# An RWKV block and an FP4 feed-forward on one Trainium2 core: chunks of 256 instead of 512 tokens

## The chip, the cores and the metric

The kernel runs on one core of a Trainium2 chip. The metric is the device time of one launch in microseconds (us). Several executions are timed and their median is given; one further execution is recorded by the hardware profiler.

## The reference

4,096 tokens (16 sequences of 256) go through three layers, all in fp32. `x` holds token numbers below 31,999; the lookup `w0[inputs]` is clipped to the 8,000 rows.

```python
# embedding
emb = einsum('blk,kh->blh', w0[inputs], w1) * (inputs != 0) * 256**0.5      # w0 8000x512, w1 512x256
# attention-like layer (D = 256, FF = 1024), after an extra layer norm of its input
h = layer_norm(x); hx = token_shift(h)
k, v, r = (h*mix + hx*(1-mix)) @ wk, wv, wr ; r = sigmoid(r)
wkv = scan over the 256 tokens of a sequence, two numerators and a running maximum
x = x + (r * wkv) @ wo
h = layer_norm(x); hx = token_shift(h)
kk = square(relu(mixed_k @ cwk)); rr = sigmoid(mixed_r @ cwr)
x = x + rr * (kk @ cwv)
# feed-forward with blockwise FP4 rounding of activations and weights, I = 704
xn = layer_norm(x)
x = x + fp4(silu(fp4(xn) @ fp4(w_gate).T) * (fp4(xn) @ fp4(w_up).T)) @ fp4(w_down).T
```

Every block of 16 values is scaled by its largest value and rounded to the 8 magnitudes of FP4.

## The kernel before

The tokens are cut into 8 chunks of 512 (two sequences, 4 tiles of 128 rows). A chunk passes three stages. Stage **a** gathers rows by indirect DMA (POOL, L429), transposes them (L497), multiplies by `w1` (L509), normalises (statistics on VectorE L949/L952, coefficients on POOL L434 to L458, application on ScalarE), transposes again (L519), forms the shifted mixes (ScalarE L744, then VectorE L963), projects to k, v, r (L537) and runs the recurrence: VectorE's scans and products (`wkv_a`, L970 to L1074, steps `a_wkv1` to `a_wkv4`) between ScalarE's relu, exp and ln (`exponentials`, L770). Stage **b** multiplies by `wo` (L557), adds (L1082), normalises, mixes, splits the key input into a high and a low fp32r part (L813, L1097), does the key matmul in three fp32r passes of 512 columns (L573), relu and square (L825, L828), gate (L835) and value (L588, run by L546). Stage **c** normalises, rounds to FP4 (`quantise`, L337: seven VectorE passes, of which the fifth, L362, waits for a square that ScalarE makes after the fourth, L358), transposes (L601), does gate and up in fp32r (L615), Silu and product (L859, L1145), rounds again, transposes (L629) and multiplies by the down weights (L642, the last 64 of 704 rows as a block of its own).

Each engine executes its own queue in order, and semaphores tie the queues together. The order of each queue is written by hand as a table `ORDER` (L67): a list of (step, lag). `walk` (L121) goes through the table once per chunk and calls each step for chunk t minus its lag; a stage-c step of chunk i thus stands beside stage-a steps of chunk i+2 or i+3. PSUM banks are handed out in a fixed cycle of jobs (`Jobs`, L131), two banks for each stage. Most tiles exist once; `h1` and the row numbers exist twice. At the start the weights of gate, up and down are themselves rounded to FP4 on VectorE (`quant_w`, L1165, three steps), transposed and split, among the first chunks' steps.

ScalarE has one table of functions at a time. Sigmoid, Silu, Exp and Ln each come with ACT_TABLE_LOAD instructions in the profile (53 in the chunks).

Of the kernel before, what the change touches and what calls it, by code (L numbers as in the profile page):

```python
# [26 lines left out]
F32 = mybir.dt.float32  # L27
F32R = mybir.dt.float32r
# [6 lines left out]
P = 128  # L35
# [8 lines left out]
GP = 88  # L44
GJ = INTER // GP
KI = 6
TAIL = INTER - (KI - 1) * P
BLOCK = 16
TOKENS = SEQS * T
CHUNK = 512  # L50
CHUNKS = TOKENS // CHUNK
NT = TOKENS // P
TILES = CHUNK // P
CS = CHUNK // T
# [5 lines left out]
AHEAD = 2  # L60
# [32 lines left out]
class Chunk:  # L93
# [15 lines left out]
class Signal:  # L109
# [6 lines left out]
    def count(self, ch, n):  # L116

        return ch.times(self.per, AHEAD * self.per + n)


def walk(name, steps):  # L121

    lags = [lag for order in ORDER.values() for _, lag in order]
    for t in range(min(lags), CHUNKS + max(lags)):
        for step, lag in ORDER[name]:
            ch = Chunk(t - lag)
            if ch.exists() and not (step[0] == "w" and ch.base > 0):
                steps[step](ch)


class Jobs:  # L131


    def __init__(self, jobs, full, emptied):
        self.names, self.who = [n for n, _ in jobs], [w for _, w in jobs]
        self.full, self.emptied = full, emptied

    def slot(self, name):
        return self.names.index(name) % 2

    def emptied_by(self, k):

        return self.emptied[self.who[k]], sum(w == self.who[k] for w in self.who[:k + 1])

    def wait_free(self, pe, ch, name):

        k = self.names.index(name) - 2
        signal, n = self.emptied_by(k % len(self.names))
        pe.wait_ge(signal.sem, signal.count(ch if k >= 0 else ch.back(1), n))

    def wait_full(self, engine, ch, name):

# [1076 lines left out]
```

## Time and profile before

| | |
|---|---|
| time of 3 runs, median (lowest to highest) | 788.66 us (787.74 to 792.24) |
| profiled execution: time, span in the trace | 790.58 us, 788.8 us |
| mean granted TensorE clock | 0.952 of full speed |
| busy: TensorE, its weight loads, VectorE, ScalarE, POOL | 89%, 72%, 76%, 65%, 19% |
| DMA moved | 19.34 MB, 25 GB/s mean |
| chain that ended last | TensorE 69%, VectorE 15%, ScalarE 7%, issue 6%, DMA 2% |

Busy time is time in which an engine has an instruction in execution. Matmuls overlap, so the distance between their starts, not their duration, is what a matmul costs. On VectorE and ScalarE two instructions that don't depend on each other overlap by some tens of nanoseconds, while one that needs the result of the one before starts after its end. The chain lists, in order of time, the pieces of work that each released the next.

### The profile page before, as it was taken

To read this page: it belongs to the slowest core of one execution; us is meant where nothing else is said; L and a number is where in the kernel's file an instruction comes from. 1 tells how busy PE (TensorE), PEld (TensorE's weight loads), DVE (VectorE), ACT (ScalarE), POOL (GpSimd) and SP (SyncE) were. 2 spreads that over 40 slices of the span, in tenths; PEclk is the share of its full clock that TensorE was granted. 3 is DMA by queue.
4 is the path that set the end of the run, shared out by engine and by line. 5 is a ranking of instruction groups with operands and counts; after the bars stand their busy time and mean duration, and the time that the engine had idled before them with its cause. 6 is when DMAs were issued, how large, how long until landed. Compare 5 with 4: busy or idle time off the path is not lost.

```text
span 788.8 us, 9882 instructions
## 1 busy us (share of the span) xinstructions
PE 698.7 (89%) x3311; PEld 566.1 (72%) x3311; DVE 600.1 (76%) x1023; ACT 511.7 (65%) x889; POOL 147.8 (19%) x220
## 2 busy tenths in 40 slices
PE   3353699699999999999999999999999999799686
PEld 2231576589688977888688958897789778688574
DVE  0797835987788888788788778888878888863763
ACT  1267488668874887389757886588748974761221
POOL 2042230433023300421022302330131003100000
PEclk9677799899999999999999999999999999899988
DMA  5800000000010000100010001000100000000000
GB/s 133 230 27 25 3 27 0 28 1 27 1 41 14 26 3 14 41 1 27 14 34 8 28 14 27 15 28 0 35 20 1 1 14 15 1 0 14 15 0 27
DMA packets 11956, 19.34 MB, mean 25 GB/s; under 512 B 972, under 2 KB 9346, under 8 KB 11906
## 3 DMA queue, kind: packets, MB, share of 16 engines
q1 hardware_dynamic: 9302, 10.31, 4.5%
q0 software_dynamic: 2560, 8.39, 3.7%
q8 instruction: 27, 0.44, 0.2%
q14 instruction: 23, 0.19, 0.1%
q10 hardware_dynamic: 44, 0.01, 0.0%
HBM read 14.51 MB, written 4.19 MB: 24 GB/s over the span
## 4 chain that ended last, share of the span: by engine, by line
PE 69%; DVE 15%; ACT 7%; issue 6%; DMA 2%; POOL 0%; SPq 0%; DVEq 0%; ACTq 0%; POOLq 0%
PE psB L546 17%; PE psB L573 11%; PE psC L642 11%; PE psC L615 11%; PE psA L537 9%; PE psA L509 3%; PE psC L629 3%; ACT mix L796 2%; DMA kkT<-L_ffn_w_gate 2%; DVE top L352 1%; DVE mix L1082 1%; PE psB L519 1%; PE psA L519 1%; DVE top L949 1%; ACT take L790 1%
## 5 line engine op out<-in xcount | busy, mean ns | idle before, releaser
L546 PE MATMUL psB<-cwv_s,kkT 128*128 128x256 f32 x512 | 113.2, 379 | 0.0
L546 PEld LDWEIGHTS psB<-cwv_s,kkT 128*128 128x128 f32 x512 | 96.6, 190 | 16.0 <-issue 3.7
L642 PE MATMUL psC<-downT,hqT 128*128 128x256 f32 (+1 forms) x384 | 97.0, 398 | 0.0
L429 POOL DMA_INDIRECT rows<-L_tok_w,ids_now x32 | 45.7, 1427 | 266.7 <-PE psA L497 255.1
L615 PE MATMUL psC<-up_hi,xq_hi 128*128 128x352 f32 x256 | 88.3, 345 | 7.4 <-DVE xq_lo L1194 6.8
L642 PEld LDWEIGHTS psC<-downT,hqT 128*128 128x128 f32 (+1 forms) x384 | 70.2, 193 | 26.7 <-issue 19.0
L537 PE MATMUL psA<-mix,kvr_s 128*128 128x512 f32 x192 | 86.8, 596 | 1.5 <-DVE mix L963 1.3
L615 PE MATMUL psC<-up_hi,xq_lo 128*128 128x352 f32 x256 | 84.0, 328 | 0.0
L615 PE MATMUL psC<-up_lo,xq_hi 128*128 128x352 f32 x256 | 83.9, 328 | 0.0
L537 PEld LDWEIGHTS psA<-mix,kvr_s 128*128 128x128 f32 x192 | 35.8, 190 | 41.1 <-issue 38.4
L963 DVE SCALAR_TENSOR_TENSOR mix<-hT,rest,mix 128x512 f32<-128x512 f32 x80 | 54.3, 747 | 10.3 <-ACT mix L744 10.3
L509 PE MATMUL psA<-w_s,rowsT 128*128 128x256 f32 x256 | 61.2, 395 | 0.0
L615 PEld LDWEIGHTS psC<-up_hi,xq_hi 128*128 128x128 f32 x256 | 49.3, 193 | 10.1 <-DVE xq_lo L1194 8.0
L573 PE MATMUL psB<-key_hi,cwk_hi 128*128 128x512 f32 x128 | 54.3, 424 | 1.9 <-ACT rr L835 1.9
L509 PEld LDWEIGHTS psA<-w_s,rowsT 128*128 128x128 f32 x256 | 50.6, 201 | 7.1
L362 DVE SCALAR_TENSOR_TENSOR hq<-square,hq 128x704 f32<-128x704 f32 x32 | 28.6, 893 | 35.1 <-ACT square L873 35.1
L744 ACT ACTIVATE mix<-hT,par 128x512 f32<-128x512 f32 x80 | 51.1, 734 | 0.2
L573 PE MATMUL psB<-key_lo,cwk_hi 128*128 128x512 f32 x128 | 50.7, 396 | 0.0
L573 PE MATMUL psB<-key_hi,cwk_lo 128*128 128x512 f32 x128 | 50.6, 395 | 0.0
L615 PEld LDWEIGHTS psC<-up_hi,xq_lo 128*128 128x128 f32 x256 | 49.3, 192 | 0.8
L546 PE MATMUL psB<-wo_s,rT 128*128 128x256 f32 x128 | 34.1, 415 | 17.1 <-DVE rT L985 17.1
L615 PEld LDWEIGHTS psC<-up_lo,xq_hi 128*128 128x128 f32 x256 | 49.2, 192 | 0.0
(163 smaller groups left out, 1435.6 us busy)
## 6 DMA issues: line engine op xcount, KB each, us to landing
out<-h SPq DMA_DIRECT2D x16, 256.0 KB, 2.1
mix<-L_attn_cwk SPq DMA_DIRECT2D x1, 1024.0 KB, 15.7
cwv_s<-L_attn_cwv SPq DMA_DIRECT2D x1, 1024.0 KB, 16.0
kkT<-L_ffn_w_gate SPq DMA_DIRECT2D x1, 704.0 KB
kkT<-L_ffn_w_up SPq DMA_DIRECT2D x1, 704.0 KB
hqT<-L_ffn_w_down SPq DMA_DIRECT2D x1, 704.0 KB, 17.9
w_s<-L_tok_w SPq DMA_DIRECT2D x1, 512.0 KB, 4.0
rows<-L_tok_w,ids_now POOLq DMA_INDIRECT x32, 4.1
```

Of the source, the lines that this page charges most:

```text
L362: op = nc.vector.scalar_tensor_tensor(out=data, in0=w.bitcast(F32), scalar=MAGIC, in1=data, op0=ALU.add, op1=ALU.add)
L429: pool.indirect_dma_start(rows[:, q, :], None, tok_w0, bass.IndirectOffsetOnAxis(ap=ids_now[:, s, t:t + 1], axis=0)).then_inc(rows_in[q], 16)
L509: mm = nc.tensor.matmul(psA[:, A.slot(f"e{j}"), q * D:(q + 1) * D], rowsT[:, q, k, :], w1_s[:, k, :], start=(k == 0), stop=(k == KE - 1))
L519: mm = nc.tensor.transpose(ps(jobs.slot(name))[:, t * P:(t + 1) * P], src[:, t, d * P:(d + 1) * P], ident[:])
L537: mm = nc.tensor.matmul(psA[:, A.slot(f"{name}{d}")], kvr_s[:, w, k, d * P:(d + 1) * P], mix[:, w, k].rearrange("p c t -> p (c t)"), start ...
L546: mm = nc.tensor.matmul(psB[:, B.slot(name), q * D:(q + 1) * D], lhsT[:, k, (2 * j + q) * P:(2 * j + q + 1) * P], weight[:, k, :], start=( ...
L573: mm = nc.tensor.matmul(psB[:, B.slot(f"kk{m}")], a[:, k, m * P:(m + 1) * P], b[:, k], start=(k == 0 and p == 0), stop=(k == H - 1 and p = ...
L615: mm = nc.tensor.matmul(psC[:, C.slot(name), f, 0:INTER // 2], a[:, k, t * P:(t + 1) * P], b[:, w, k, f * (INTER // 2):(f + 1) * (INTER // ...
L629: mm = nc.tensor.transpose(psC[0:n, C.slot(name), k // 4, (k % 4) * P:(k % 4 + 1) * P], hq[:, t, k * P:k * P + n], ident[:])
L642: mm = nc.tensor.matmul(psC[:, C.slot(name), 0, q * D:(q + 1) * D], hqT[0:n, q, k, :], downT[0:n, k, :], start=(k == 0), stop=(k == KI - 1))
L744: nc.scalar.activation(dst[:, w, d], src[:, d, :, 1:ROW], ACT.Identity, scale=col(m, d)).then_inc(sig.sem, 1)
L963: nc.vector.scalar_tensor_tensor(out=dst[:, w, d], in0=src[:, d, :, 0:T], scalar=rest[:, PARAMS.index(m) - MIXES, d:d + 1], in1=dst[:, w, ...
```

## The change

A chunk is now one sequence of 256 tokens (2 tiles of 128), and there are 16 of them. Many tiles exist twice, one for even and one for odd chunks (`rows`, `h0`, `y`, `hT`, `mix`, `rT`, `hT2` and the statistics), `h1` four times; `norm`, `x1`, `e_new`, `numer`, the statistics and the scales have tiles of their own. `ORDER` holds, for each engine, every step with its chunk, from the first to the last.

Where a step was done once for each half of D (128 channels) on 512 columns, most are done once for both halves on 2 x 256 columns: all of the recurrence but `top`, `now`, `rise` and `fall`. Steps with a scalar for each channel stay one instruction for each half and are half as wide (mixes, affine, `rise`, `fall`). Rows padded from 704 to 768 (zeros) make the down matmuls all 128 rows deep, and one copy replaces three after the transposes. Key matmuls stream 256 columns, and the two passes with the same stationary block stand next to each other. The weights are rounded in 6 parts of 128x704 in two steps each (`w_scale`, `w_round`) in place of 3 steps, and gate and up are loaded by rows of 128 values. `exponentials` asks for the table with both Exp and Ln by name.

```diff
-CHUNK = 512
-CHUNKS = TOKENS // CHUNK
+CHUNK = T
+CHUNKS = SEQS
 UNROLL = 2
+KEPT = 4
...
 ORDER = {
     "pe": """
...
+        c_cols.7 a_cols.10 b_out.9 c_up0.7 a_k.10 c_turn1.6 a_v.10 b_cols.9 c_down.6 c_up1.7 a_r.10 b_key0.9
+        a_turn0.11 c_turn0.7 a_turn1.11 a_emb.11 b_key1.9 b_key2.9 b_key3.9 b_gate.9 b_value.9
...
     "act": """
...
+        c_cols.7 a_y.10 a_cols.10 a_part.10 c_up0.7 b_norm.9 a_k.10 a_v.10 c_sq0.7 c_turn1.6 b_cols.9 b_part.9
+        a_wkv1.10 c_up1.7 b_high.9 a_wkv2.10 a_r.10 a_turn0.11 c_sq1.7 a_turn1.11 c_turn0.7 b_key0.9 c_norm.8
+        a_emb.11 b_key1.9 b_key2.9 b_key3.9 b_gate.9 c_sqn.8 a_wkv3.10 a_norm.11
...
     "dve": """
+        w_par.0 a_stat.0 w_scale0.0 w_scale1.0 w_round0.0 a_mix.0 w_round1.0 w_key.0 a_wkv1.0 w_split0.0
...
+        b_x1.9 a_mix.10 c_stat.8 c_up0.7 c_quant0.7 a_wkv1.10 c_down.6 b_mix.9 b_low.9 c_up1.7 c_quant1.7
+        a_wkv2.10 a_wkv3.10 a_stat.11 c_norm.8 a_wkv4.10 b_value.9 c_split.8
...
     "pool": """
+        gather.0 gather.1 a_coef.0 a_coef.1 b_sum.0 b_coef.0 gather.2 a_coef.2 c_coef.0 b_sum.1 b_coef.1
...
-A_JOBS = [("xt0", "act"), ("xt1", "act"), ("e0", "act"), ("xt2", "act"), ("xt3", "act"), ("e1", "act"),
-          ("n0", "act"), ("n1", "act")] + [(f"{w}{d}", "act") for w in "kvr" for d in range(H)]
+A_JOBS = [("xt0", "act", 0), ("xt1", "act", 0), ("e", "act", 0), ("n", "act", 0), ("k", "act", 0), ("v", "act", 0),
+          ("r", "act", 0)]
...
+def reloads(ch):
+    order = places("act")
+    a, b = order.index(("a_wkv1", ch.base)), order.index(("a_wkv3", ch.base))
+    return ["rise0"] + ["log"] * any(step in ("a_r", "b_gate", "c_up0", "c_up1") for step, _ in order[a:b])
...
             def exponentials(ch, names):
+                if names[0] in reloads(ch):
+                    nc.scalar.preload_act_table_set(LOG_EXP)
...
-                            for p, (a, b) in enumerate(((cwk_hi, key_hi), (cwk_lo, key_hi), (cwk_hi, key_lo))):
-                                mm = nc.tensor.matmul(psB[:, B.slot(f"kk{m}")], a[:, k, m * P:(m + 1) * P], b[:, k],
+                            for p, (a, b) in enumerate(((cwk_hi, key_hi), (cwk_hi, key_lo), (cwk_lo, key_hi))):
+                                mm = nc.tensor.matmul(psB[:, B.slot(ch, name), q * T:(q + 1) * T], a[:, k, m * P:(m + 1) * P],
...
-            nc.scalar.copy(dst[:, 0:4, :], ps[:, slot, 0].rearrange("p (k n) -> p k n", k=4))
-            nc.scalar.copy(dst[:, 4, :], ps[:, slot, 1, 0:P])
-            nc.scalar.copy(dst[0:TAIL, 5, :], ps[0:TAIL, slot, 1, P:2 * P]).then_inc(last, 1)
+            nc.scalar.copy(hqT[:, t], six(psC[:, C.slot(ch, name)])).then_inc(c_act, 1)
...
             for k, w in enumerate((w_gate, w_up)):
-                sp.dma_start(raw_up[:, k * GJ:(k + 1) * GJ, :], w.rearrange("(j p) d -> p j d", p=GP))
+                sp.dma_start(raw[k], w.rearrange("n (h d) -> (n h) d", h=H).rearrange("(j p) d -> p j d", p=P))
```

The SP queue now waits for the rows of chunk 1 as well before it issues the loads of gate and up, and issues `cwk` ahead of `w_down`.

## Rows read from the trace of the kernel before

**Rows 1.** The page's part 1: busy us, share of the span, instructions.
```profile
PE 698.7 (89%) x3311; PEld 566.1 (72%) x3311; DVE 600.1 (76%) x1023; ACT 511.7 (65%) x889; POOL 147.8 (19%) x220
```

**Rows 2.** Busy by stage: length, PE, PEld, DVE, ACT, POOL, granted clock, DMA share, GB/s.
```profile
0.00:50.00 50.00, 15.76 (x64) 12.80 (x65) 26.75 (x43) 12.91 (x21) 13.41 (x29) 0.77 0.58 150
...
300.00:400.00 100.00, 99.25 (x482) 80.50 (x482) 83.87 (x143) 74.25 (x129) 18.27 (x27) 1.00 0.06 19
...
750.00:789.00 39.00, 29.54 (x132) 24.06 (x132) 19.32 (x27) 7.28 (x17) 0.00 (x0) 0.85 0.04 14
```

**Rows 3.** The chain that ended last: start us, us, what.
```profile
245.38 1.29 DVE mix L1082 x2
...
259.65 3.84 PE psC L615 x24
...
271.44 2.81 PE psB L573 x12
...
294.88 5.77 PE psC L642 x24
...
304.28 6.91 PE psB L546 x32
...
666.82 1.29 DVE mix L1082 x2
...
777.67 7.76 PE psC L642 x24
```

**Rows 4.** Timeline of VectorE: start us, us, instruction, count, idle before.
```profile
338.71 0.89 DVE L352 TENSOR_REDUCE top<-hq 128x44 f32<-128x704 f32 x1
...
340.32 0.89 DVE L358 SCALAR_TENSOR_TENSOR hq<-hq,top 128x704 f32<-128x704 f32 x1
342.14 0.89 DVE L362 SCALAR_TENSOR_TENSOR hq<-square,hq 128x704 f32<-128x704 f32 x1 [0.93 <-ACT square L873]
...
344.80 0.68 DVE L1194 TENSOR_TENSOR xq_lo<-psC,xq_hi 128x512 fp32r<-128x512 f32 x1
...
366.66 4.06 DVE L963 SCALAR_TENSOR_TENSOR mix<-hT,rest,mix 128x512 f32<-128x512 f32 x6
370.63 0.89 DVE L1145 TENSOR_TENSOR hq<-psC,hq 128x704 f32<-128x704 f32 x1
...
395.92 0.69 DVE L1111 TENSOR_TENSOR rr<-psB,rr 128x512 f32<-128x512 f32 x1
396.64 0.69 DVE L1113 TENSOR_TENSOR h<-h,rr 128x512 f32<-128x512 f32 x1
...
400.95 1.28 DVE L988 TENSOR_TENSOR mix<-mix,take 128x512 f32<-128x512 f32 x2
```

**Rows 5.** Timeline of ScalarE, columns as in rows 4.
```profile
357.03 1.28 ACT L859 ACT_TABLE_LOAD   x1
358.32 0.76 ACT L859 ACTIVATE hq<-psC 128x704 f32<-128x704 f32 x1
358.98 1.08 ACT L825 ACTIVATE kkT<-psB 128x512 f32<-128x512 f32 x2
...
380.82 1.33 ACT L790 ACTIVATE keep<-take,decay 128x512 f32<-128x512 f32 x2 [0.71 <-DVE take L988]
382.06 1.32 ACT L790 ACTIVATE take<-take,decay 128x512 f32<-128x512 f32 x2
383.40 1.28 ACT L790 ACT_TABLE_LOAD   x1
384.69 1.15 ACT L790 ACTIVATE keep<-keep 128x512 f32<-128x512 f32 x2
```

**Rows 6.** Timeline at the start: the load of gate, and the key weights' split.
```profile
12.72 0.46 SPq L385 DMA_DIRECT2D kkT<-L_ffn_w_gate  x1
...
24.76 2.35 DVE L352 TENSOR_REDUCE hq<-kkT 88x64 f32<-88x1024 f32 x2 [17.51 <-DMA kkT<-L_ffn_w_gate]
...
61.05 2.29 DVE L1102 TENSOR_TENSOR cwk_lo<-mix,cwk_hi 128x2048 fp32r<-128x2048 f32 x1
```

More of the change, by code:

```diff
@@ L116, in count, with places @@
     def count(self, ch, n):
-        return ch.times(self.per, AHEAD * self.per + n)
+        return ch.base * self.per + n
+def places(name):
+    return [(step, int(base)) for step, base in (entry.split(".") for entry in ORDER[name].split())]
 def walk(name, steps):
[L123 to L128, printed above, removed]
+    for step, base in places(name):
+        steps[step](Chunk(base))
@@ L165 @@
-C_JOBS = [("q0", "dve"), ("g0", "act"), ("u0", "dve"), ("q1", "dve"), ("g1", "act"), ("u1", "dve"),
-          ("hq0", "act"), ("g2", "act"), ("u2", "dve"), ("hq1", "act"), ("g3", "act"), ("u3", "dve"), ("d0", "dve"),
-          ("hq2", "act"), ("hq3", "act"), ("d1", "dve")]
-WKV = ["pad"] + [f"{step}{d}" for step in ("top", "gain", "now", "takev", "sumv", "sum1", "newv", "numer", "denom",
-                                           "near", "fix", "avg", "att")
-                 for d in range(H)]
@@ L174 @@
-EXPS = [f"{step}{d}" for step in ("rise", "fall", "keep", "take", "new", "log", "inv") for d in range(H)]
-QUANT = 7
+        if ch.exists():
+            self.emptied_by(engine, self.place[name, ch.base])
+A_JOBS = [("xt0", "act", 0), ("xt1", "act", 0), ("e", "act", 0), ("n", "act", 0), ("k", "act", 0), ("v", "act", 0),
+          ("r", "act", 0)]
+B_JOBS = [("o", "dve", 0), ("t", "act", 0), ("kk0", "act", 0), ("kk1", "act", 0), ("kk2", "act", 0), ("kk3", "act", 0),
+          ("rr", "act", 0), ("cv", "dve", 0)]
@@ L345, in wide @@
                 return t.unsqueeze(2).to_broadcast([p, nb, BLOCK])
-            for stage in range(QUANT):
+            for stage in stages:
                 for k, (data, w, big, scale, p, nb) in enumerate(parts):
@@ L502, in emb @@
-            def emb(j):
-                def step(ch):
-                    A.wait_free(pe, ch, f"e{j}")
+                    if ch.base == 0 and t == 0:
+                        pe.wait_ge(s_idc, 1)
+                    pe.wait_ge(rows_in[ch.parity][t], 16 * (ch.base // UNROLL + 1))
+                    A.wait_free(pe, ch, f"xt{t}")
+                    for k in range(KE):
+                        mm = nc.tensor.transpose(psA[:, A.slot(ch, f"xt{t}"), k * P:(k + 1) * P],
+                                                 rows[:, ch.parity, t, k * P:(k + 1) * P], ident[:])
@@ L778, in exponentials @@
                         "keep": (k, k, ACT.Exp, -1.0, 0.0),
                         "take": (t, t, ACT.Exp, -1.0, 0.0),
-                        "new": (n, n, ACT.Exp, 1.0, 0.0),
+                        "new": (e_new[:], e_new[:], ACT.Exp, 1.0, 0.0),
                         "log": (t, k, ACT.Ln, 1.0, 0.0),
                         "inv": (t, t, ACT.Exp, -1.0, 0.0),
-                    }[step]
-                    made = {"rise": "gain", "fall": "now", "new": "now", "log": "denom"}
-                    before = {"fall": "rise", "keep": "rise", "take": "fall", "inv": "log"}
@@ L786, in exponentials @@
-                    if step in made:
-                        at(act, wkv, ch, WKV.index(f"{made[step]}{d}") + 1)
-                    if step in before:
-                        at(act, wkv_exp, ch, EXPS.index(f"{before[step]}{d}") + 1)
+                    }[name.rstrip("01")]
+                    made = {"rise0": "gain", "fall0": "now0", "fall1": "now1", "log": "denom"}
+                    earlier = {"fall0": "rise0", "fall1": "rise1", "keep": "rise1", "take": "fall1", "inv": "log"}
+                    if name in made:
+                        at(act, wkv, ch, WKV.index(made[name]) + 1)
@@ L975, in expd @@
                     at(dve, wkv_exp, ch, EXPS.index(name) + 1)
-                def both(where, fn):
-                    if part == where:
-                        for d in range(H):
-                            fn(d).then_inc(wkv.sem, 1)
-                now, before = slice(1, ROW), slice(0, T)
                 def stt(out, in0, scalar, in1, op0, op1):
-                    return nc.vector.scalar_tensor_tensor(out=out, in0=in0, scalar=scalar, in1=in1, op0=op0, op1=op1)
+                    nc.vector.scalar_tensor_tensor(out=out, in0=in0, scalar=scalar, in1=in1, op0=op0, op1=op1).then_inc(wkv.sem, 1)
@@ L1006, in wkv_a @@
-                both(1, f_top)
-                def f_gain(d):
-                    after(f"top{d}")
-                    return tt(take[:, d, :, now], kT[:, d], top[:, d, :, before], ALU.subtract)
-                both(1, f_gain)
-                def f_now(d):
-                    after(f"gain{d}")
-                    A.wait_full(dve, ch, "k1")
-                    return nc.vector.tensor_scalar(e_new[:, d], take[:, d, :, now], col("time_first", d), BEYOND,
-                                                   ALU.add, ALU.min)
@@ L1175, in quant_w, with round_w, step @@
+                    quantise_w(j, range(SCALED))
+                return step
+            def round_w(j):
+                def step(_):
+                    quantise_w(j, range(SCALED, QUANT))
                 return step
```

1102 lines of the change are left out of this document (578 added, 524 removed), and 18 rows, old and new, of the table ORDER.

## The prediction

> **What bounds the kernel now.** I read the busy shares first [rows 1]: TensorE 89%, VectorE 76%, ScalarE 65%. A mean over a kernel with a long start and end says little, so next came the table by stage [rows 2]: between 300 and 400 us TensorE is busy 99.25 of 100 us at clock 1.00, in the first 50 us only 15.8, in the last 39 only 29.5 at clock 0.85. The chain [rows 3] shows the rhythm: the same addition (L1082) at 245.38 and at 666.82 is five chunks apart, so a chunk of 512 takes 421.4/5 = 84.3 us. Eight of them are 674 us; the other 115 us of the 788.8 us span are start and end. Two things can move the time: the period, and that 115 us. The VectorE timeline [rows 4] shows that VectorE isn't far behind: it is busy 83.87% of the steady stretch [rows 2], and also stands still within `quantise`, 0.93 us in a pass over 704, because it waits for ScalarE's square and nothing in its queue may overtake.
>
> **TensorE's part of the period.** Distances between starts come from the chain [rows 3]: 3.84/24 = 0.160 us for fp32r with 352 columns, 2.81/12 = 0.234 us with 512 columns, 6.91/32 = 0.216 us for fp32 with 256 columns.
> - fp32 matmuls: number and columns in total stay, or pairs of half the columns take the place of one: nil.
> - Down: 24 instructions take 5.77 us, at 0.216 they'd be 5.19; the 64-row block is what they have and others don't. Made 128 deep they save 0.58 us for 256 tokens.
> - Key: 96 matmuls of 256 columns for each 512 tokens in place of 48 of 512. Both fp32r rows lie 9% above columns / 2.4 GHz (0.147 and 0.213), so 256 columns give 0.1165 us, and 96 x 0.1165 = 11.2 us, the same as 48 x 0.234. Bounds: 0.107 (columns alone), a gain of 0.5 us a chunk of 256; 0.160 (no cheaper than 352), a loss of 48 x 0.0435 = 2.1 us. I take 0.1165, between rows that agree.
> - Same stationary block twice in a row: nil; weight loads already hide (80.5 us busy of 100 beside matmuls at 99) [rows 2].
>
> Now TensorE has about 0.6% idle, so its sum for 256 tokens is 84.3 x 0.993/2 - 0.58 = 41.3, rounded to 41.0 to 41.5.
>
> **VectorE's part.** Half of 83.87% of 84.3 us is 35.4 us. The waits for squares (two of 0.93, one of about 0.8) add 2.6. Mixes: six of 512 take 370.63 - 366.66 = 3.97 us, 0.66 each; at 1.04 ns an element (the 0.20 us between 704 and 512 elements: 0.89 and 0.69) half of one is 0.40, so ten cost 4.0 instead of 5 x 0.66 = 3.3: +0.7. The recurrence: today its two halves alternate, so that a step starts 0.59 us after the other (two in 1.28 us, each 0.69); with both halves in one instruction each step needs the one before, and the distance is 396.64 - 395.92 = 0.72. Seven such steps: +0.9. Other ends of dependent steps, about 0.5. Sum 40.1 us.
>
> **ScalarE's part.** Half of 74.25% is 31.3 us. Halved affine, mix, `rise`, `fall` cost more starts, one copy for three gives some back: +1. Table loads: today 53, or 3.3 for 256 tokens. After, the order for one chunk reads `a_wkv1` (named table), `c_up1` (Silu), `a_wkv2` (Exp), `a_r` (Sigmoid), `a_wkv3` (named table), `c_up0` (Silu): 6 loads, +2.7 x 1.28 = 3.5. Sum 35.8 us. The load asked for ahead of `rise0` is thrown away, since Silu stands before the first Exp.
>
> A load takes 1.28 us and the next instruction starts 0.01 us after it (357.03 + 1.28, next at 358.32) [rows 5]. The Trainium skill (ScalarE: Activation LUTs, What ACT_TABLE_LOAD costs) adds a drain of 1.38 us, 2.66 in all, to each switch; this trace shows no such gap, so the sum goes by 1.28.
>
> **How the queues tie.** No engine's own sum passes 41.3, but VectorE waits for ScalarE once more. When `gain` of a chunk is done, ScalarE runs: four `rise`/`fall` at 256 (0.62 apart at 512, less 0.21 each: 1.75 with the end), load 1.28, Silu 0.65, `b_high` 0.6, load 1.28, three exps 1.7, load 1.28, sigmoid 0.5, `a_turn0` 0.45, and then the square `c_sq1` 0.8: 10.3 us [rows 5]. VectorE in that time has `now` 0.6, `c_down` 0.6, `b_mix` 1.6, `b_low` 0.6, `c_up1` 0.9, the first four passes 2.5 (344.80 - 338.71 is the whole with 0.93 of waiting) [rows 4], and would have its square at 7.7. It waits 2.6 us more. Behind `a_wkv3` (load, ln, exp after `c_sqn`) `a_wkv4` waits another 0.5. Period: 40.1 + 3.1 = **43.3 us** for 256 tokens, 86.6 for 512 against 84.3 now. The bound moves from TensorE to VectorE and ScalarE together. TensorE then has 2 us idle a chunk, which also holds its wait for `a_r` before `a_turn1`.
>
> **Start and end.** VectorE's whole queue, in order: first weight pass at 27 (now 24.8 [rows 6], gate is issued some 2.2 us later, behind the rows of chunk 1; `a_stat.0` fits before). Weights: six parts of 5.2, `cwk_lo` 2.3 [rows 6], splits 3.6: 37. Sixteen chunks: 642. Twelve steady periods with 3.2 of coupling: 38. Waits while the pipeline fills, where ScalarE must take `w_sq` before `a_cols`: bounds 0 and 25, I take 10. At the end VectorE waits for the last gates and values: 13 (bounds 5 and 20), and behind the last quantise come transposes, a copy, half a down block, the addition and the store: 8 (now the last down block alone is 7.76 for twice the tokens at the lower clock [rows 3]). Sum 27 + 37 + 642 + 38 + 10 + 13 + 8 = 775; with rounding of the parts 775 to 778, say 777 us span. The profiled execution was 790.6 for a span of 788.8, and the median of the runs 788.66, so about the span: **777 us**, -1.5%. In short: 512 tokens cost 2.3 us more in the steady part, and start and end (788.8 - 674 = 115) shrink to about 777 - 16 x 43.3 = 84. Gathers and stores (32 and 16 as now, POOL and SP queues) stay hidden: POOL is busy 18 of 100 us [rows 2], and double rows let gathers go earlier.
>
> **Rivals.**
> 1. *TensorE stays the bound.* If ScalarE's chain is shorter, or VectorE reaches its square later by what it waited elsewhere, the period is 41.2: 777 - 12 x 2.1 = 752, or less with a short start. For it: VectorE's own sum is below TensorE's. Against: the three loads in that chain are in the queue in this order.
> 2. *Slower: ScalarE's chain becomes the cycle.* `rise0` is reached only about 0.1 us before `gain` is; ahead of it stand `c_sq0`, `c_turn1`, `b_cols`, `b_part` and the thrown-away load, all behind VectorE's own fourth pass. Every us that ScalarE is later there adds a us to the period. The point of decision is 1.3 us a chunk: 777 + 12 x 1.3 = 792.6. At 46 us it's 809. For it: six loads, three engines between 36 and 41. Against: ScalarE has 7 us of idle to give.
> 3. *fp32r with 256 columns costs 0.160.* TensorE needs 43.4, with some wait for the others 44.3: 789, no change. Against: both rows scale with columns.
> 4. *The start is longer by 10.* Gate comes in rows of 512 bytes, half as long as now, and `a_cols.0` waits behind `w_sq0`: 787, no change.
> 5. *A drain at each load.* By a gap of 1.38 us after the loads, the four in the chain add 5.5 us: 843. The row with 0.01 us speaks against it. (It is the rule of the Trainium skill named above.)
>
> That the change doesn't do what it says is possible for the repeated stationary block (two loads still); that costs nothing.
>
> **How the numbers follow.** Forecast 44% (its own range 763 to 786), rival 1 20%, rival 2 20%, rival 3 7%, rival 4 7%, rival 5 2%. About 0.5% (3.9 us) is what a measurement of this kernel can tell from no change. Faster: rival 1 and most of the forecast, 62%; same: rivals 3, 4 and the forecast's upper edge, 14%; slower: rival 2, rival 5, edges, 24%. Range 746 to 806: to the middle of rival 1 and of rival 2, which leaves out some 20%.
>
> **What would show it.** Right: the additions `b_x1` 43.3 us apart; TensorE busy near 95% in the steady part, with gaps before `a_turn1`; VectorE idle some 3.5 us before its fifth pass in `c_quant1`, put down to ScalarE's square; 96 loads or so; down matmuls 0.216 apart throughout; key matmuls 0.117 apart. Wrong: TensorE at 99% (rival 1), a period over 44.6 with ScalarE over 90% busy (rival 2), key matmuls at 0.16 (rival 3), the first weight pass after 30 us (rival 4).

## The result and the profile after

The changed kernel takes **812.3 us** (median of 4 runs, 808.51 to 813.58), the kernel before beside it 788.2 us (787.34 to 792.24): a ratio of 1.028, 95% interval 1.0256 to 1.0309. It is slower by 24 us. The prediction was 777 us (746 to 806), faster: wrong in sign, and the result lies outside the range. The profiled execution took 811.32 us for a span of 809.5 us.

The page's part 1 of the changed kernel, which answers to [rows 1]:

```profile
PE 706.7 (87%) x3877; PEld 628.5 (78%) x3877; DVE 628.4 (78%) x1112; ACT 601.2 (74%) x1001; POOL 163.9 (20%) x336
```

ScalarE has gained most, 90 us of busy time, and TensorE's share has fallen. In the table by stage (columns as in [rows 2]) the steady part looks like this:

```profile
400.00:500.00 100.00, 96.62 (x552) 86.50 (x550) 84.61 (x157) 84.56 (x142) 28.15 (x52) 1.00 0.07 21
```

TensorE was busy 99.25 of 100 us before [rows 2] and is now 96.62: it waits, at clock 1.00. How long a chunk of 256 takes is read from the addition `b_x1`, once as a group (first and last start of 16) and once in the timeline (the fourth, chunk 3):

```profile
L1107 DVE TENSOR_TENSOR x<-psB,y x16: 681/692/693, 60.9 to 710.4; 128x512 f32<-128x512 f32 x16
...
182.56 0.69 DVE L1107 TENSOR_TENSOR x<-psB,y 128x512 f32<-128x512 f32 x1
```

From the fourth to the sixteenth are twelve periods: (710.44 - 182.56) / 12 = **43.98 us** (predicted 43.3; before, 84.3 / 2 = 42.15 [rows 3]). What is left of the span, 809.5 - 16 x 43.98, is start and end: **105.8 us** (predicted 84; before 115). These two numbers hold the whole miss: 16 x 0.68 = 11 us, and 22 us.

ScalarE's table loads as groups of instructions (line, count | busy us, mean ns | idle before). L868 is the load that the kernel asks for by name, L945 Silu's, L861 the sigmoid of `a_r`, L887 the exps':

```profile
L868 ACT ACT_TABLE_LOAD x31 | 39.8, 1283 | 0.5
L945 ACT ACT_TABLE_LOAD x28 | 35.9, 1283 | 8.6 <-PE psC L721 8.1
L861 ACT ACT_TABLE_LOAD x15 | 19.2, 1283 | 1.0 <-PE psA L654 0.7
L887 ACT ACT_TABLE_LOAD x12 | 15.4, 1283 | 0.2
```

With three of `b_gate` and one at the start that is 90, against 54 before by the same count. Where they stand shows the profile's chain through one period (start us, us, what; "..." stands for pieces left out):

```profile
411.38 5.18 PE psC L746 x24
416.56 1.94 PE psC L721 x12
...
418.59 0.49 ACT take L887
...
420.39 0.76 ACT hq L945
...
421.67 0.94 ACT L887
...
424.66 1.28 ACT L861
425.96 0.60 ACT rT L861
...
426.70 0.63 PE psA L616 x4
...
430.87 4.25 PE psB L690 x36
435.11 8.64 PE psB L663 x40
...
444.63 1.99 PE psB L663 x8
```

The chain alone misleads here, and the timelines of ScalarE and VectorE show what it leaves out:

```profile
416.03 1.28 ACT L868 ACT_TABLE_LOAD   x1
417.37 0.91 ACT L887 ACTIVATE keep<-take,decay 128x256 f32<-128x256 f32 x2
...
426.91 0.80 ACT L956 ACTIVATE square<-hq 128x704 fp32r<-128x704 f32 x1
```

```profile
416.64 0.69 DVE L1056 TENSOR_TENSOR take<-kT,top 128x512 f32<-128x512 f32 x1
...
421.69 0.69 DVE L1118 TENSOR_TENSOR key_lo<-mix,key_hi 128x512 fp32r<-128x512 f32 x1 [1.52 <-ACT key_hi L907]
...
427.83 0.89 DVE L485 SCALAR_TENSOR_TENSOR hq<-square,hq 128x704 f32<-128x704 f32 x1 [2.12 <-ACT square L956]
...
443.88 0.69 DVE L1053 SCALAR_TENSOR_TENSOR rT<-numer,rT 128x512 f32<-128x512 f32 x1
...
446.76 0.69 DVE L1107 TENSOR_TENSOR x<-psB,y 128x512 f32<-128x512 f32 x1 [0.26 <-PE psB L663]
```

Read them as a loop. VectorE's `gain` (L1056) ends at 417.33, the load ahead of `rise0` at 417.31. From there ScalarE doesn't stand still: `rise` and `fall`, Silu's table and Silu, `key_hi`, the exps' table and the exps, the sigmoid's table and `a_r` (done at 426.56), a copy of `a_turn0`, and the square `c_sq1` (done at 427.71), 10.4 us in all. The chain enters this stretch from TensorE's gates, but these end at 418.50, and Silu's load starts at 419.10, when `fall` is done; they don't hold it up.

Two paths leave the stretch. TensorE gets its bank for `a_turn1` from `a_r`; it has waited 1.53 us. VectorE gets its square from `c_sq1`. They meet at `b_out`, the product with `wo` (444.63), which needs VectorE's last step of the recurrence, `att` (L1053). `att` ends at 444.57, 0.06 us ahead of it. Between 200 and 680 us this distance is 0.05 or 0.06 us in ten of eleven periods. TensorE's last transposes ahead of it start at 444.02 and the ones before them took 0.43, so TensorE alone could have begun some 0.17 us earlier (an estimate from these starts). VectorE closes the loop, and TensorE's path is only just shorter. From one `b_x1` (402.92) to the next (446.76): 14.41 us on VectorE to `gain`, 10.38 on ScalarE, 16.86 on VectorE to `att`, 2.19 for `b_out`, together 43.84. (The mean of 43.98 holds two early periods of 44.5.)

The groups of waits of VectorE from 403 to 447 us:

```profile
DVE hq L485 <- ACT square L956: 3.0, 2, 2.1
DVE key_lo L1118 <- ACT key_hi L907: 1.5, 1, 1.5
DVE normc L485 <- ACT square L951: 0.8, 1, 0.8
```

### The profile page after: what moved, and what is told of

The parts are those of the page before. It is cut to its first block, busy times and chain, and to the rows that moved or that the text cites. A ratio compares the mean times of both kernels' runs of the same rounds, so it can differ in the third digit from the quotient of the medians.

```text
span 809.5 us, 11541 instructions
## 1 busy us (share of the span) xinstructions
PE 706.7 (87%) x3877; PEld 628.5 (78%) x3877; DVE 628.4 (78%) x1112; ACT 601.2 (74%) x1001; POOL 163.9 (20%) x336
## 4 chain that ended last, share of the span: by engine, by line
PE 50%; ACT 20%; DVE 20%; issue 8%; DMA 1%; POOL 1%; DVEq 0%; ACTq 0%; POOLq 0%; SPq 0%
PE psB L663 13%; PE psC L721 9%; PE psC L746 7%; PE psA L654 7%; PE psB L690 5%; PE psA L628 4%; ACT take L887 3%; ACT L861 2%; ACT L868 2%; DVE hq L485 2%; DVE hq L488 2%; PE psC L736 2%; ACT keep L887 1%; ACT L887 1%; DVE mix L1038 1%
## 5 line engine op out<-in xcount | busy, mean ns | idle before, releaser
L654 PE MATMUL psA<-mix,kvr_s 128*128 128x256 f32 x384 | 97.7, 402 | 16.7 <-DVE mix L1038 16.7
L654 PEld LDWEIGHTS psA<-mix,kvr_s 128*128 128x128 f32 x384 | 75.2, 203 | 28.1 <-DVE mix L1038 18.9
L746 PE MATMUL psC<-downT,hqT 128*128 128x256 f32 x384 | 87.7, 386 | 0.4 <-DVE hq L1152 0.4
L721 PE MATMUL psC<-up_lo,xq_hi 128*128 128x352 f32 x256 | 84.3, 329 | 0.0
L721 PE MATMUL psC<-up_hi,xq_lo 128*128 128x352 f32 x256 | 84.3, 329 | 0.0
L746 PEld LDWEIGHTS psC<-downT,hqT 128*128 128x128 f32 x384 | 73.1, 194 | 10.8 <-DVE hq L1152 1.1
L690 PE MATMUL psB<-key_hi,cwk_hi 128*128 128x256 f32 x256 | 76.4, 298 | 3.8 <-DVE key_lo L1118 3.1
L1038 DVE SCALAR_TENSOR_TENSOR mix<-hT,rest,mix 128x256 f32<-128x256 f32 x160 | 72.6, 517 | 0.6 <-ACT mix L840 0.6
L690 PE MATMUL psB<-key_hi,cwk_lo 128*128 128x256 f32 x256 | 71.9, 281 | 0.0
L690 PE MATMUL psB<-key_lo,cwk_hi 128*128 128x256 f32 x256 | 71.9, 281 | 0.0
L840 ACT ACTIVATE mix<-hT,par 128x256 f32<-128x256 f32 x160 | 67.5, 497 | 3.1
L721 PEld LDWEIGHTS psC<-up_hi,xq_hi 128*128 128x128 f32 x256 | 49.6, 194 | 17.3 <-DVE h L1166 9.0
L690 PEld LDWEIGHTS psB<-key_hi,cwk_hi 128*128 128x128 f32 x256 | 48.8, 191 | 8.5 <-DVE key_lo L1118 7.5
```

The source lines that it names most:

```text
L654: mm = nc.tensor.matmul(psA[:, A.slot(ch, name), d * T:(d + 1) * T], kvr_s[:, w, k, d * P:(d + 1) * P], mix[:, ch.parity, w, k], start=(k ...
L690: mm = nc.tensor.matmul(psB[:, B.slot(ch, name), q * T:(q + 1) * T], a[:, k, m * P:(m + 1) * P], b[:, k], start=(k == 0 and p == 0), stop= ...
L721: mm = nc.tensor.matmul(psC[:, C.slot(ch, name), f, 0:INTER // 2], a[:, k, t * P:(t + 1) * P], b[:, w, k, f * (INTER // 2):(f + 1) * (INTE ...
L746: mm = nc.tensor.matmul(psC[:, C.slot(ch, "d"), 0, q * D:(q + 1) * D], hqT[:, q, k, :], downT[:, k, :], start=(k == 0), stop=(k == KI - 1))
L840: nc.scalar.activation(dst[:, w, d], src[:, d, 1:ROW], ACT.Identity, scale=col(m, d)).then_inc(sig.sem, 1)
L1038: nc.vector.scalar_tensor_tensor(out=dst[:, w, d], in0=src[:, d, 0:T], scalar=rest[:, PARAMS.index(m) - MIXES, d:d + 1], in1=dst[:, w, d], ...
```

## The experiments

Two theories stood at the beginning. A: ScalarE's table loads, by where the written-out order puts them, make ScalarE late for the engines that wait in the steady loop. B: the halved instructions themselves cost too much on VectorE (or TensorE), and the waits only show its slack. sq1_early, load_hidden, tanh_gates, tail_warm and key_order start from no_rise_load; tanh_warm starts from tanh_gates; no_tables, rise_silu, rise_silu2 and fill_no_tables from the changed kernel. The edits are cut to what they change; "..." marks what is left out. Beside the experiments the kernel before, run on the same chip, took 789.6 to 790.4 us; differences between experiments of 2 us and more mean something.

### Without the load ahead of rise0 (no_rise_load)

```diff
-    return ["rise0"] + ["log"] * any(...)
+    return ["log"] * any(...)
```

> The changed kernel without the table load that is asked for ahead of rise0. Since Silu (c_up1) stands before the first exp, this load is thrown away, and without it Silu of c_up1 finds the table of c_up0 still there: 4 loads a chunk in place of 6, some 55 in all for 86. Theory A (in the steady part VectorE waits for ScalarE's square and key_hi, because ScalarE needs 10.3 us from gain to c_sq1, loads in it): one load of 1.28 us leaves that stretch and one stands before it, so the period falls by 1.3 to 2.4 us from 43.9, to 41.5 to 42.6, VectorE's wait in c_quant1's fifth pass from 2.1 to under 1 us, and the time by 12 to 16 of these, to 780 to 796. Theory B (the halved instructions themselves made VectorE slower, 37.1 us busy a chunk, and the waits are only where its slack shows): no change, 809 to 815. Theory C (TensorE's own cost rose): no change either.

Measured: 790.96 us (789.25 to 791.79), ratio to before 1.0009 (0.9999 to 1.0018). A single line gives back 21 us. Its additions:

```profile
L1107 DVE TENSOR_TENSOR x<-psB,y x16: 684/692/692, 60.3 to 689.8; 128x512 f32<-128x512 f32 x16
```

The fourth came at 180.58, so the period is 509.3 / 12 = 42.44 us. Theory A's time and period hold. Two of its numbers don't: 62 of the 86 loads are left and not 55, and VectorE's wait in the fifth pass of `c_quant1` did not shrink (2.0 us for 2.1). Silu's reload, which went with it, stood ahead of `key_hi`, so `key_lo`'s wait of 1.5 us is gone; VectorE reaches its fourth pass earlier, and the square comes about as much earlier. TensorE's wait before `a_turn1` fell too, from 1.5 us a time (16.6 us in 11 waits between 200 and 700 us) to 0.24 (2.6 in 11). `b_out` still starts 0.05 to 0.06 us after `att` in ten of eleven periods: the same loop, 1.4 us shorter. And ScalarE now waits 1.36 us for `gain` before `rise0`, which shows that `gain` is where its stretch begins.

### Without any table load (no_tables)

```diff
-    return ["rise0"] + ["log"] * any(...)
+    return ["rise0"] if ch.base == 0 else []
...
-ACT.Sigmoid, ACT.Silu
+ACT.Relu
```

> The changed kernel with Relu in the place of Sigmoid and Silu, and the table with Exp and Ln loaded once: sigmoid and silu are left out of the computation, the number and size of the instructions stay. No table load is left in the steady part (6 x 1.28 us of ScalarE a chunk go). Theory A: TensorE is the bound again with its own sum of 41.0 to 41.5 us a chunk; time 812 minus 12 x 2.6, minus the loads that stood on the chain in the start and the end (about 8 us): 767 to 780, TensorE at 98% or more in the steady part. Theory B: VectorE's busy time of 37.1 us is untouched and the period stays over 43: 800 or more. If it lands between, the waits have another source beside the loads.

Measured: 772.12 us (771.14 to 773.51), ratio 0.978 (0.9761 to 0.9795). In the steady part:

```profile
400.00:500.00 100.00, 99.54 (x590) 91.22 (x590) 87.82 (x157) 71.98 (x135) 23.73 (x47) 1.00 0.05 17
```

Additions from 171.88 to 670.2: 41.53 us a period. TensorE is the bound again, at the sum that the prediction gave it (41.0 to 41.5); `b_out` now starts some 0.25 us after `att`. Theory B falls: VectorE's instructions are all still there. The start became 10.7 us shorter too, where about 8 had been expected of start and end together.

### The square ahead of the sigmoid (sq1_early)

```diff
-c_up1.7 b_high.9 a_wkv2.10 a_r.10 a_turn0.11 c_sq1.7 a_turn1.11
+c_up1.7 b_high.9 a_wkv2.10 c_sq1.7 a_r.10 a_turn0.11 a_turn1.11
```

> As no_rise_load, and in ScalarE's queue c_sq1 stands right behind a_wkv2, ahead of a_r and a_turn0 of the next chunk (11 chunks). VectorE's wait for this square then goes to nothing (it has to be 1.28 + 0.5 + 0.45 us earlier), but a_r comes 0.8 us later or more, and TensorE needs its bank for a_turn1. Theory A with VectorE as the tied engine: 0 to 8 us less than no_rise_load. Rival (the cycle passes through a_r to TensorE's a_turn1 and a_emb): 5 to 12 us more than no_rise_load, with TensorE's wait before a_turn1 longer by about a us a chunk.

Measured: 809.17 us (808.32 to 810.47), 18 us more than no_rise_load. The rival was right in sign and too small in size. The period is 43.88 us, 1.44 more. The groups of waits from 404 to 448 us, and `att` and `b_out` in the timelines of VectorE and TensorE, show who pays:

```profile
PE psA L616 <- ACT rT L861: 2.2, 1, 2.2
...
DVE hq L485 <- ACT square L956: 1.9, 2, 0.9
```

```profile
444.37 0.69 DVE L1053 SCALAR_TENSOR_TENSOR rT<-numer,rT 128x512 f32<-128x512 f32 x1
...
445.96 1.89 PE L663 MATMUL psB<-wo_s,rT 128*128 128x256 f32 x8
```

VectorE's wait for the two squares of `c_quant` fell from 3.0 to 1.9 us, as intended; TensorE's wait for `a_r` rose from 0.24 to 2.2. From `gain` to the end of `a_r` it is now 9.8 us (418.30 to 428.06) for 7.8, since the square itself takes 0.8 and ScalarE first waits 1.2 us for VectorE's fourth pass. `b_out` starts 0.9 us after `att` and no longer 0.06: now TensorE's path closes the loop. The experiment shows that the two paths lie close, so that time taken from one at the cost of the other is lost. It does not show that VectorE's wait was off the loop before. (The wait for the square of `normc` rose from 0.8 to 2.8 us too: ScalarE comes late to everything behind TensorE's delay.)

### The load ahead of rise0 kept, Silu's reload gone (rise_silu, rise_silu2)

```diff
-                    nc.scalar.preload_act_table_set(LOG_EXP)
+                    nc.scalar.preload_act_table_set(LOG_EXP if names[0] == "log" else SILU)
```

> The changed kernel with its load ahead of rise0 kept, but of the table with Silu, which is there already: c_up1's Silu then needs no load of its own. It parts the 21 us that no_rise_load gained. Theory A: the load ahead of rise0 ends just when gain does (417.31 and 417.33 us in the profile of the changed kernel), so it costs nearly nothing, and it is Silu's reload, in the stretch from gain to c_sq1, that costs 1.3 us and more a chunk: 790 to 798. Rival (the load ahead of rise0 makes ScalarE late, rival 2 of the prediction): it keeps its half or more, 800 to 808.

Measured: 803.66 us (803.15 to 804.14), where the rival expected it. But the additions say otherwise: 191.2 for the fourth and 702.7 for the last, 42.63 us a period against 42.44 without this load. The 10 us were lost in the start, where no Silu stands between `rise0` and the exps, so that this table was the wrong one. The edit was therefore kept to chunks 3 to 14:

```diff
+                    nc.scalar.preload_act_table_set(LOG_EXP if names[0] == "log" or not 3 <= ch.base < 15 else SILU)
```

> As rise_silu, but in chunks 0 to 2 and 15, where no Silu stands between rise0 and the exps, the load ahead of rise0 is that of the changed kernel. rise_silu had 42.63 us between additions in the steady part (no_rise_load 42.44, the changed kernel 43.98), but reached the fourth addition at 191.2 (180.6, 182.6). Theory A (the load ahead of rise0 costs 0.2 us a chunk, Silu's reload 1.35): fourth addition at 182 to 184, 12 x 42.6 behind it, 792 to 797 in all. Rival (the load ahead of rise0 makes ScalarE late): 800 to 808 again.

Measured: 792.29 us (790.22 to 795.16), fourth addition at 181.51, 42.62 us a period. So of the 21 us of no_rise_load about 1 belongs to the load ahead of `rise0`, and 20 to the reload that Silu then needs behind it. The first ends when `gain` does; the second stands in ScalarE's stretch behind it, from which both paths leave.

### Two thrown-away loads elsewhere (load_hidden)

```diff
+                    if name == "v" and ch.base > 3:
+                        nc.scalar.preload_act_table_set(SILU)
                     A.wait_full(act, ch, name)
...
+                if 1 < ch.base < CHUNKS - 3:
+                    nc.scalar.preload_act_table_set(LOG_EXP)
                 C.wait_full(act, ch, "q")
```

> no_rise_load with two thrown-away loads a chunk put elsewhere: one ahead of a_v, where ScalarE waits 1.9 us for TensorE anyway (chunks 4 on), one ahead of c_cols, where it waits 1.6 us (chunks 2 to 12). Loads and ScalarE's busy time are those of the changed kernel again, only their place differs. Theory A (a load costs by where it stands: 21 us for two a chunk at rise0 and c_up1): 790 to 796. Rival (ScalarE's busy time as such sets the period, rival 2 of the prediction): 808 to 814.

Measured: 793.67 us (792.5 to 795.0), 2.7 us more than no_rise_load, with 42.7 us a period. In the steady part ScalarE is busier than in the changed kernel:

```profile
400.00:500.00 100.00, 98.91 (x562) 89.07 (x561) 87.52 (x159) 87.31 (x147) 26.03 (x50) 1.00 0.08 25
```

87.31 of 100 us, and 19 us less time. ScalarE's busy share was never the bound; the place of two loads was.

### Sigmoid by tanh (tanh_gates)

```diff
-ACT.Sigmoid if name == "r" else ACT.Copy
+ACT.Tanh if name == "r" else ACT.Copy, scale=0.5 if name == "r" else 1.0
...
-stt(attT[:, ch.parity], numer[:], -1.0, rT[:, ch.parity], ALU.mult, ALU.mult)
+stt(attT[:, ch.parity], rT[:, ch.parity], 1.0, numer[:], ALU.add, ALU.mult)
...
-nc.vector.tensor_tensor(flat(x1), psB[...], flat(y[...]), ALU.add)
+nc.vector.scalar_tensor_tensor(out=flat(x1), in0=psB[...], scalar=-0.5, in1=flat(y[...]), op0=ALU.mult, op1=ALU.add)
```

`b_gate` is changed in the same way, with its two products on VectorE.

> The changed kernel without the load ahead of rise0, and both sigmoids written as (1 + tanh(x/2))/2: tanh and exp may lie in one table, the 1 goes into the product that follows and the 1/2 into the next addition, with as many instructions as before. The load ahead of a_r falls away, a third of the stretch from gain to c_sq1, and one load a chunk less (3 in place of 4). Theory A: without that load ScalarE is no longer late for VectorE's square nor for TensorE's a_turn1, TensorE bounds at its own 41.3 to 41.5 us a chunk as it did without any table load: 12 x 0.9 us less than no_rise_load (42.4 a chunk) and 2 to 8 us less in the start: 772 to 779. If the last loads cost nothing (no_tables gained by the cheaper functions), 787 to 792. If tanh needs a table of its own, there are more loads, not fewer, and the time is over 795.

Measured: 779.85 us (778.43 to 784.05), ratio 0.9875 (0.983 to 0.9919). The load groups show that tanh needs no table of its own behind the exps (L887), and the three loads a chunk:

```profile
L868 ACT ACT_TABLE_LOAD x15 | 19.2, 1283 | 0.3
L887 ACT ACT_TABLE_LOAD x15 | 19.2, 1283 | 0.3
L945 ACT ACT_TABLE_LOAD x15 | 19.2, 1283 | 5.0 <-PE psC L721 4.8
```

Fourth addition at 174.97, last at 678.7: 41.98 us a period, 0.46 less than no_rise_load where 0.9 was expected, so that the time came out just above the 772 to 779 expected. TensorE doesn't bound here yet: `b_out` still starts 0.05 to 0.06 us after `att`. The start gave 5.6 us. That exp and tanh lie in one set is what the Trainium skill says (ScalarE: Activation LUTs, Table sets: the hidden batching unit), and the trace agrees. The same section puts 2.7 us to a load; here it is 1.28 and the next instruction follows 0.01 us later.

### Loads added to the kernel before (before_loads, before_hidden)

```diff
                 def step(ch):
+                    if t % 2:
+                        nc.scalar.preload_act_table_set("natural_log_exp_and_others")
                     C.wait_full(act, ch, f"g{t}")
```

> The kernel before with a thrown-away load ahead of every second Silu (c_up1, c_up3): two of them and two reloads for 512 tokens more than now, some 32 in all, about half of what the changed kernel has too much. Here TensorE is the bound at 99% and ScalarE has 21 us of idle in a chunk of 84. Theory A: they cost next to nothing, 788 to 794. Rival (every load on ScalarE shows in the time, 32 x 1.28 = 41 us, or half of it): 805 to 830.

Measured: 812.21 us (811.31 to 814.07), ratio 1.027 (1.0235 to 1.0309). Theory A as I had put it missed: a bound TensorE doesn't make ScalarE's loads free. The additions went from 84.3 to (685.71 - 248.73) / 5 = 87.4 us apart for 512 tokens, and in TensorE's timeline a wait stands behind the late Silu (the next longest, 0.6 us, is for `kkT`):

```profile
356.29 0.85 PE L629 MATMUL psC<-ident,hq 128*128 128x128 f32 x6 [1.73 <-ACT hq L861]
```

So the same four loads for 512 tokens went to where ScalarE waits 5.56 us anyway:

```diff
+                    if j == 0:
+                        for name in ("silu_and_others", "natural_log_exp_and_others") * 2:
+                            nc.scalar.preload_act_table_set(name)
                     C.wait_full(act, ch.back(1), f"u{2 * j + 1}")
```

> The kernel before with four thrown-away loads a chunk of 512 ahead of c_cols0, where ScalarE waits 5.56 us for TensorE. That is as many more loads as in before_loads (32 in all, 41 us of ScalarE), which cost 22 us ahead of two of the Silus. If a load costs by what waits behind it, here too: 788 to 793. If it was the number of loads: 805 to 815.

Measured: 791.83 us (789.84 to 793.32), ratio 1.003 (1.0014 to 1.0044). In the timeline of VectorE, the third and the eighth addition:

```profile
250.13 1.28 DVE L1085 TENSOR_TENSOR mix<-psB,y 128x512 f32<-128x512 f32 x2
...
671.62 1.28 DVE L1085 TENSOR_TENSOR mix<-psB,y 128x512 f32<-128x512 f32 x2
```

421.49 / 5 = 84.30 us, exactly that of the kernel before. Thirty-two loads in a wait cost nothing in the steady part (in this execution the second addition, at 160.94 before, is at 164.49, so the 2 us of the median lie in the start), and 22 us in front of Silu.

### The down blocks made full, in the kernel before (before_pad)

```diff
+            nc.vector.memset(downT[TAIL:P, KI - 1, :], 0.0).then_inc(s_pad, 1)
...
-                            n = P if k < KI - 1 else TAIL
-                            mm = nc.tensor.matmul(..., hqT[0:n, q, k, :], downT[0:n, k, :], ...)
+                            mm = nc.tensor.matmul(..., hqT[:, q, k, :], downT[:, k, :], ...)
...
-                    turned(psC, C.slot(name), hqT[:, t % 2], c_act.sem)
+                    nc.scalar.copy(hqT[:, t % 2], psC[:, C.slot(name)]...[:, 0:WIDE]...).then_inc(c_act.sem, 1)
```

> The kernel before with one part of the change alone: the down matmuls 128 rows deep in all six blocks (zero rows in the weights), and one copy in place of three after the transposes. By the step of the prediction a 64-row block costs 0.58 us for 256 tokens more than a full one, and TensorE bounds this kernel at 99%: 16 x 0.58 = 9.3 us less, 778 to 781. Rival (the distance in the down stretch has another reason, or the gain is given back as a wait): 786 to 790.

Measured: 781.93 us (781.8 to 784.01), ratio 0.990 (0.9879 to 0.9912). A line of its chain, beside the 5.77 us of [rows 3]:

```profile
380.19 5.18 PE psC L642 x24
```

0.59 us for 256 tokens, and 83.24 for 84.29 us a period. This part of the change is good by itself, and the changed kernel has it too (5.18 in its chain above).

### The order of the key passes (key_order)

```diff
-for p, (a, b) in enumerate(((cwk_hi, key_hi), (cwk_hi, key_lo), (cwk_lo, key_hi))):
+for p, (a, b) in enumerate(((cwk_hi, key_hi), (cwk_lo, key_hi), (cwk_hi, key_lo))):
```

> no_rise_load with the three key passes in the order of before, so that the same stationary block no longer stands twice in a row. By the prediction that part of the change is worth nothing: within 2 us of no_rise_load (789 to 793), 36 key matmuls in 4.1 to 4.3 us as now. Rival (a repeated block saves its weight load): 36 in 5 us or more, and 5 us or more on the time.

Measured: 790.92 us (789.23 to 792.38), 0.04 less than no_rise_load. 36 key matmuls take as long as in the changed kernel (4.25 in its chain):

```profile
380.26 4.24 PE psB L690 x36
```

### The start without loads (fill_no_tables)

```diff
+    if ch.base <= 3:
+        return ["rise0"] * (ch.base == 0)
...
-ACT.Sigmoid if name == "r" else ACT.Copy
+(ACT.Relu if ch.base <= 3 else ACT.Sigmoid) if name == "r" else ACT.Copy
```

The same for `b_gate` up to chunk 2 and for Silu in chunk 0.

> The changed kernel with no table load among the steps of chunks 0 to 3 that stand ahead of the fourth addition: Relu in the place of Sigmoid (a_r of chunks 0 to 3, b_gate of 0 to 2) and of Silu (c_up of chunk 0), which leaves these functions out for these chunks; all later chunks as in the changed kernel. The fourth addition came at 182.6 us in the changed kernel and at 171.9 in no_tables. If the loads are what the start costs too much: fourth addition at 171 to 174, 8 to 11 us less in all, 801 to 805. If no_tables gained them otherwise, or they are given back behind: 809 to 814.

Measured: 800.64 us (800.37 to 801.42), ratio 1.014 (1.0114 to 1.017). The fourth addition in VectorE's timeline:

```profile
173.64 0.69 DVE L1109 TENSOR_TENSOR x<-psB,y 128x512 f32<-128x512 f32 x1
```

8.9 us earlier than in the changed kernel, and the time is 11.7 less. The loads among the first chunks' steps are on the path there. That they are so because each chunk still runs from engine to engine with nothing beside it is argued, not tested.

### TensorE's clock in the end (tail_warm, tanh_warm)

```diff
+            def warm(n):
+                A.wait_emptied(pe, Chunk(CHUNKS - 1), "r")
+                for k in range(n):
+                    nc.tensor.matmul(psA[:, k % 2, 0:D], ident[:], w1_s[:, 0, :], start=True, stop=True)
```

> no_rise_load with 64 matmuls of 256 columns that nobody reads, put where TensorE stands still in the last 40 us: 40 ahead of c_cols of the last chunk (it waits 11.6 us there), 24 ahead of its c_turn1 (6.6 us). They ask whether the end is long because of TensorE's clock: in the profile of no_rise_load the last gates come 0.29 us apart and not 0.16, and the last 24 down matmuls take 7.06 and not 5.2 us. If the granted clock stays up through them, 5 to 6 us less than no_rise_load: 784 to 787. If the clock doesn't follow, or the end is set by the walk between the engines alone: 790 to 793.

Measured: 795.16 us (793.58 to 795.8), 4 us more than no_rise_load. I had counted an fp32 matmul as one instruction; it is two, so that the chain shows 80 and 48 of them:

```profile
737.87 17.27 PE psA L708 x80
...
772.21 10.36 PE psA L708 x48
```

They took 17.3 and 10.4 us, where the waits held 11.6 and 6.6: 9.5 us too long, for a time only 4.2 us longer. The stretch from 735 us on was at clock 1.00, for 0.78 without them, so the question stayed, with fewer of them and on top of tanh_gates:

> tanh_gates with the matmuls that nobody reads in the end, now as many as the waits hold. In tail_warm each of them ran as two instructions of 0.216 us, 80 and 48, took 17.3 and 10.4 us where the waits are 11.6 and 6.6, and the last stretch was at clock 1.00 for 0.78. Now 26 and 15 (11.2 and 6.5 us). If the clock makes the end longer, 5 to 6 us less than tanh_gates: 773 to 776. If the end is set by the walk between the engines alone: 779 to 781.

Measured: 778.19 us (776.81 to 778.84), ratio 0.9852 (0.9823 to 0.9881), the lowest median of the kernels that leave nothing out. In the chain of tanh_gates the last transposes of `normc`, the gates behind them and the last down matmuls are

```profile
739.17 1.13 PE psC L637 x4
...
741.81 5.79 PE psC L721 x24
...
766.71 6.58 PE psC L746 x24
```

and in that of tanh_warm

```profile
743.73 0.67 PE psC L637 x4
...
745.91 4.12 PE psC L728 x24
...
768.48 5.20 PE psC L755 x24
```

From the first of these transposes to the last addition (773.31 and 773.70 us) it is 34.1 us against 30.0: the clock is worth 4.2 us there. The medians differ by 1.7 us only, and the ranges touch (778.43 to 784.05 and 776.81 to 778.84), so that the gain in time isn't shown. The two profiled executions are the fastest of one and nearly the slowest of the other: in tanh_warm the stretch began 4.6 us later. Of that 3.0 us stood already at the fourth addition (177.99 for 174.97), which the edit doesn't reach, and 1.6 in 24 gates ahead of the added matmuls (5.68 us at clock 0.70 for 4.12 at 1.00). The 5 to 6 us expected were too much.

## Why the prediction was wrong

**What held.** The loop of the steady part (below). TensorE's own work, 41.0 to 41.5 us a chunk: 41.53 with no table load. Key matmuls at 256 columns, 0.1165 us: 4.24 / 36 = 0.118. The full down block, 0.58 us: 0.59. The repeated stationary block, nil. VectorE's instructions, 35.4 + 0.7 + 0.9 = 37.0 us: 84.61% of 43.98 is 37.2, and 36.76 in the period from 402.92 us on. Six loads a chunk, each 1.28 us with nothing behind it (rival 5 is out). Rival 3 is out. Rival 4 is out in the form given: the first weight pass began at 20.4, not after 30. (ScalarE's sum was too low, 35.8 us for 37.4, but no other number hung on it.)

**The steady part: the right loop, 0.7 us too short.** "How the queues tie" took the stretch from `gain` over Silu, the exps and the sigmoid to `c_sq1` as 10.3 us; it is 10.38. It ended it at VectorE's square, and VectorE does close the loop, 0.06 us ahead of `b_out`. It put VectorE's wait beyond the usual 0.93 at 2.6; it is 1.52 + 1.19 = 2.7, in two places. `a_wkv4` waits 0.39 for 0.5. And it laid TensorE's wait for `a_r` into 2 us of idle that cost nothing: TensorE is idle 1.7 of 43.84 us, 1.53 of them there. What was mis-sized is the sum 40.1 + 3.1. Of the 43.84 us VectorE is busy 36.76 and waits 5.99; the other 1.09 are short gaps behind dependent steps, which the sum had at "about 0.5". And `b_x1` waits 0.26 for `b_out`, which it had at nothing. What the sum didn't see is the margin: TensorE's path is only some 0.2 us shorter, and sq1_early pays for that.

Rival 2 did not come true as it was put: the thrown-away load ahead of `rise0` costs 0.2 us a chunk (42.62 for 42.44). The reload behind it costs 1.36 (43.98 - 42.62), but that the forecast had in its stretch, as Silu's 1.28. So the reload is why the changed kernel is slow, and not why the forecast missed.

**Start and end: 84 predicted, 105.8 measured, the larger part of the miss.** This is the step that failed. Its terms:
- "Waits while the pipeline fills ... I take 10" (bounds 0 and 25). From 20.4 us to the fourth addition VectorE's waits sum to 29.5 us. Some 6.3 of them are for squares, which the 40.1 us of each chunk hold, so about 23 stand against the 10, inside the bounds. The loads there alone cost 9 us (fill_no_tables); the term was taken without counting a single one. The early first weight pass (20.4 for 27) gave 6.6 us back.
- "At the end VectorE waits for the last gates and values: 13 (bounds 5 and 20)", and 8 behind the last quantise. VectorE stands still 44.5 us after the last `b_x1` (99.1 us long, 54.6 busy). The groups of its waits from 710.4 us on:

```profile
DVE hq L1152 <- PE psC L721: 12.1, 3, 6.8
DVE h L1166 <- PE psC L746: 8.7, 1, 8.7
DVE hq L485 <- ACT square L956: 6.6, 6, 2.0
DVE hq L1152 <- ACT hq L945: 5.8, 2, 3.4
```

Gates and Silu are 17.9 us, and with a value and a split (2.3 and 1.9) 22 for the 13; above the upper bound. The last addition waits 8.7 us, and it and the store add 3.3: 12 for the 8. The 6.8 us are 24 gates at a granted clock of 0.59: eighteen come 0.29 us apart (the level of 1.2 GHz) and the last six 0.16, as in the steady part (2.4 GHz). The sum names no clock for them; tanh_warm puts some 4 us of the last stretch to the clock. The rest is the walk between the engines with two chunks, then one, in the pipeline, and no experiment has split it further.

**The sign.** The period rose by 1.8 us for 256 tokens against before, 12 to 16 of them 22 to 29 us, and the shorter start and end (105.8 for 115) gave back 9. The forecast had foreseen a longer period; all of its gain was to come from start and end (115 to 84), on a sum of waits that no row had shown. The changed kernel loses through a reload that one line causes. Without this line it is as fast as the one before (ratio 1.0009), not faster: 42.44 us is still 0.3 above 42.15, and its start and end, 110, are 5 shorter.

**What stays of the change.** Full down blocks (-8 us in the kernel before) are worth having in either kernel. The small chunk pays only when ScalarE's stretch is short: with tanh for the sigmoids 779.85 us, faster than both kernels and by 2 us than before_pad (781.93). With TensorE kept busy in the last waits it is 778.19, too near to tell from 779.85.

## What to carry to other kernels

Ask of a table load not how long it is but which wait ends behind it: 32 of them cost nothing in one place and 22 us in another, in the same kernel. When functions of several tables alternate in a hand-written order, look for a load that the next function throws away, and for a function that lies in its neighbour's table. And where two engines wait for the same stretch, look for the place where their paths meet, and at which of them releases it: here `b_out` followed VectorE's `att` by 0.06 us, which neither the chain nor the longest wait says. Shortening the stretch that both share gave 21 us; giving one path's time to the other cost 18.

## What was not expected of the hardware

- A load of the table that is already there still takes its 1283 ns (in rise_silu2 the load of Silu's table ahead of `rise0`, where `c_up0`'s Silu has already brought it; in load_hidden the one ahead of `a_v`).
- TensorE at 99% busy had no slack for ScalarE: 2.56 us more ahead of two of four Silus cost 3.1 us in 84.3 (before_loads).
- In the last 37 us of tanh_gates TensorE is busy 25.6 us and the granted clock is 0.82; with 82 instructions that nobody reads in its waits it is 1.00 (tanh_warm, 32.2 of 38 us).
